# Two sequences per turn in place of one in TensorE's loop over the six local-attention layers

## The reference, cut to what matters

```
for i in range(DEPTH):            # DEPTH = 6, HEADS = 16, DIM_HEAD = 64, WINDOW = 32
    x = attn_layer(shift_tokens(x), Wqkv[i], q_scale[i], k_scale[i], Wo[i]) + x
    x = ffn_layer(shift_tokens(x), ln_g[i], ln_b[i], W1[i], b1[i], W2[i], b2[i]) + x
# attn_layer: qkv = x @ Wqkv; l2-normalised q, k with scaled rotary tables;
#   softmax over a window of 32 + 32 keys; (attention @ v) @ Wo
# ffn_layer: layer norm; a, gate = split(xn @ W1 + b1); (a * gelu(gate)) @ W2 + b2
```

## Time and profile before

| what | value |
|---|---|
| median of 3 executions | 4560.43 us (4554.09 to 4564.13) |
| span of the profiled execution, first to last instruction | 4548.5 us |
| TensorE's loop over the layers | 92 turns, from 1535.8 to 4461.2 us |
| TensorE busy with matmuls, over the whole span | 87% |

### The profile page before, as it was taken

How to read it: one execution, slowest core, us unless ns; L and a number is a source line. 1 busy time by engine, 2 the same in 40 slices (tenths; PEclk the granted TensorE clock), 3 DMA queues, 4 the chain that set the end, 5 groups by cost and what they waited for, 6 DMA issues and landing times. The chain is left out here.

```text
span 4548.5 us, 193033 instructions
## 1 busy us (share of the span) xinstructions
PE 3976.9 (87%) x73440; PEld 3313.4 (73%) x73441; DVE 3489.3 (77%) x6491; ACT 3343.1 (73%) x6195; POOL 2757.1 (61%) x3194
## 2 busy tenths in 40 slices
PE   7999845656556899999999999999999999999998
PEld 4555424544435788888888888888888888888886
DVE  6888352223336799999999999999999999999994
ACT  4777423333324799889998999899998999899995
POOL 3333252332235677777776777677776777677772
PEclk9999877777777999999999999999999999999999
DMA  4000322421211111121112111121112211121111
GB/s 159 1 0 0 81 86 100 149 75 63 91 42 50 46 44 51 40 71 47 44 47 61 50 50 44 45 68 45 47 48 58 55 45 44 44 68 48 47 44 39
DMA packets 141379, 254.22 MB, mean 56 GB/s; under 512 B 33984, under 2 KB 56640, under 8 KB 136640
## 3 DMA queue, kind: packets, MB, share of 16 engines
q1 hardware_dynamic: 133088, 235.11, 17.9%
q0 software_dynamic: 8192, 17.84, 1.3%
HBM read 70.38 MB, written 44.04 MB: 25 GB/s over the span
## 5 line engine op out<-in xcount | busy, mean ns | idle before, releaser
L2723 POOL TENSOR_TENSOR d_rc<-d_rc,d_rs 128x512 f32<-128x512 f32 x768 | 967.6, 1282 | 314.2 <-DVE d_rs L2806 277.3
L2733 POOL TENSOR_TENSOR d_rc<-d_rc,d_inv 128x1024 f32<-128x1024 f32 x384 | 723.1, 1904 | 127.7 <-DVE d_inv L2827 127.7
L2540 ACT ACTIVATE d_sq<-d_pair 128x512 f32<-128x512 f32 x768 | 454.3, 592 | 237.6 <-DVE d_rs L2806 141.8
L2293 PE MATMUL d_pair<-d_W_high,d_xs_high 128*128 128x512 f32 x1152 | 523.7, 455 | 96.7 <-issue 41.4
L2806 DVE TENSOR_TENSOR d_rc<-d_pair,d_rot 128x512 f32<-128x512 f32 x768 | 525.1, 684 | 15.4 <-ACT d_sq L2540 8.8
L2806 DVE TENSOR_TENSOR d_rs<-d_pair,d_rot 128x512 f32<-128x512 f32 x768 | 523.2, 681 | 0.0
L2293 PE MATMUL d_pair<-d_W_low,d_xs_high 128*128 128x512 f32 x1152 | 462.3, 401 | 1.2 <-issue 1.2
L2293 PE MATMUL d_pair<-d_W_high,d_xs_low 128*128 128x512 f32 x1152 | 461.2, 400 | 0.0
L2816 DVE TENSOR_REDUCE d_ss<-d_sq 128x16 f32<-128x1024 f32 x384 | 448.3, 1209 | 0.0
L2834 DVE TENSOR_REDUCE d_mx<-d_pair 128x16 f32<-128x1024 f32 x192 | 235.0, 1224 | 217.4 <-PE d_pair L2379 217.4
L2440 PEld LDWEIGHTS d_pair<-d_OT,d_Wo 128*128 128x128 f32 x3072 | 373.5, 192 | 18.5 <-issue 1.5
(11 more groups left out here) (404 smaller groups left out, 10362.6 us busy)
## 6 DMA issues: line engine op xcount, KB each, us to landing
d_VW<-d_V SPq DMA_DIRECT2D x768, 128.0 KB, 2.4
d_VW<-d_V SPq DMA_DIRECT2D x576, 64.0 KB, 2.0
leaf_rows<-a_zeros SPq DMA_DIRECT2D x12, 1152.0 KB, 14.6
q_xrow<-leaf_rows SPq DMA_DIRECT2D x24, 576.0 KB
leaf_out<-q_yrow SPq DMA_DIRECT2D x24, 512.0 KB, 2.6
d_W_whole<-Wqkv_dram SPq DMA_DIRECT2D x7, 1536.0 KB, 6.5
f_xrow<-leaf_rows SPq DMA_DIRECT2D x8, 576.0 KB, 3.6
b_table<-q_w_dram SPq DMA_DIRECT2D x4, 1024.0 KB, 7.9
```

Of the source, the lines that this page charges most:

```text
L2293: mm = nc.tensor.matmul(target, x_part[:, t.par, :], w_part[:, c, :], start=n == 0, stop=n == 2)
L2540: nc.scalar.activation(sq[:, half, 512 * j:512 * j + 512], ps[:, j, :], ACT.Square).then_inc(s[f"s{qk}{j}_ready"], 1)
L2723: nc.gpsimd.tensor_tensor(own[:, :, a, :], own[:, :, a, :], other[:, :, 1 - a, :], ALU.add).then_inc(s[f"add{qk}_ready"], 1)
L2733: nc.gpsimd.tensor_tensor(heads(rc[:, t.par, half, :]), heads(rc[:, t.par, half, :]), inv[:, t.par, half, :].unsqueeze(2).to_broadcast([12 ...
```

## The change

A new driver, and TensorE is run by it. The same slots run in the same order with the same waits; a turn of the loop now holds four slots in place of two, and there are 46 turns in place of 92. The eight slots ahead of the loop and the eight behind it stay as they are, and so do the drivers of the other engines.

```diff
+        def run_in_pairs(eng, slot):
+
+            def peeled(l, b):
+                for par in range(2):
+                    slot(lambda behind: Tile(l, b, par, behind))
+
+            for b in range(UNROLLED):
+                peeled(0, b)
+            with eng.Fori(UNROLLED // 2, LAYERS * SEQS // 2) as two:
+                for odd in range(2):
+                    for par in range(2):
+                        slot(lambda behind: FlatTile(two * 2 + odd, par, behind))
+            for b in range(UNROLLED):
+                peeled(LAYERS, b)
...
-            run_flat(pe, slot)
+            run_in_pairs(pe, slot)
```

## The result

The changed kernel took 5408.12 us at the median (5397.98 to 5427.45) against 4562.28 for the kernel before, beside it: a ratio of 1.186, 95% interval 1.184 to 1.1876, 846 us more. The forecast was 5190, with a range to 5290. The direction held, the size didn't: 627 us were foreseen, and 5408 lies above the range.

What follows compares the result with a forecast made beforehand. TensorE was taken to bound the layer loop. Slots +377, turn ends +293, less 6 and 17 for branches and 20 for split-weight waits, gave +627 us on the 4560 median: 5190 us, range 5000 to 5290.

Steps and rivals of the forecast that it cites:

- The bound: In the layer loop TensorE, busy for 2802 of 2886 us, sets the time; VectorE is in lock step with it.
- A: Rival: the instruction store holds the new turn, so only branches go: -6 us, 4554 us; chance 0.06.
- B: Rival: held turn as in A, VectorE's chain keeps out of the way, full 0.37 us gained: -17 us, 4543; chance 0.03.
- C: Rival: fetching is hidden inside a turn and only the branch misses: +146 us, 4706 us; chance 0.05.
- D: Rival: some packets stay, or the missed target comes with its successor: 5085, 5065 or both 4960 us; chance together 0.16.
- the head's second stop: Packet ends 14 instructions behind the loop's head, at the turn's fifth matmul: a further stop of 2.8 us.
- signs named: Expected in the new trace: 11 to 13 packets a turn, issue stops of 2 to 2.5 us, turns of about 77 us.
- 182 x 2.07 = +377 us: Loop slots running as first-time code, each 2.07 us longer from fetch stops; bounds +127 to +564 us.
- the three slots: Full slots in first-time code, 16.22, 18.62 and 17.93 us, mean 17.59 against 15.52 in the loop.
- The turn's end: At 45 taken branches to packets not held, stops of 3.75 and 2.8 us, 6.5 us together: +293 us.
- The value of a branch: At 46 removed turn ends, 0.37 us each, of which VectorE's chain takes 0.24 back: 0.13 us, 6 us in all.
- waits for split weights: At a layer's first tiles a late TensorE finds weights ready: some 4 us at five places, -20 us.

Runs made afterwards that it cites:

- the rotated kernel: The kernel before, two slots to a turn, with its loop cut mid-slot behind the turned keys so the branch hides behind issued matmuls: 4344.51 us against 4346.97, ratio 0.999.

## Why the prediction was wrong in size

**Right.** The bound, and that TensorE's stops have no cover. The mechanism: a turn of 11.3 packets is read anew each time, no packet of it stays, and the rivals with a held turn (A, B), hidden fetching (C) and packets kept by their place (D) are out: 13 of 13 touched packets came in each turn, with stops. The place of the head's second stop, to the instruction. Of the signs named, 13.0 packets to a turn came (11 to 13 foreseen); the turn is 82 us and not 77, its start has 4.8 us of stops and not 6. That a stop is a delivery less the time of the packet before.

**The term that was missing.** The prediction said of the slots "182 x 2.07 = +377 us" and priced no change of the clock at all; it took the 0.99 of the earlier trace rows along. The stops take TensorE's clock to its lower level, and the matmuls behind them cost 1.30 us a slot, +233 us. The two kernels with idle time and no fetching show that the idle time does it. The rows were read for their gaps alone. The granted clock fell to 0.50 at the last two of these stops, which end at 4475.62 and 4479.49, and stayed there for 6.8 us, as this row of the kernel before has it (the clock is the last column but two):

```profile
4478.10:4484.90 6.80, 5.35 (x51) 4.91 (x51) 2.66 (x5) 3.19 (x7) 0.00 (x0) 0.50 0.01 2
```

What hid the term is that the three slots of which the 2.07 us was taken all ran at 1.00; the stretch of the earlier trace rows around them had 0.96.

**Terms that were mis-sized.** The stops inside slots: 2.07 us a slot foreseen. Measured are 2.90 with the head's second stop, which is 1.15 us a turn or 0.29 a slot; the rest is 2.61 against the 2.07, 180 x 2.61 = 470 us against 377. The three slots that the mean came from had one stop of 0.72 us in the first, two in the second (1.16 us at 1538.48, and the one below, which the earlier trace rows leave out) and one in the third:

```profile
1553.52 0.24 PE L2412 MATMUL d_pair<-d_VW,d_PT 64*32 64x64 f32 x1 [1.82 <-issue]
```

The stop at 1538.48 is the head's second stop, and the prediction counts it twice: in the mean of the slots and again at the turn's end. Without it the mean is 2.07 - 1.16 / 3 = 1.7 us, so stops inside slots were taken too small by 0.9 us. The turn has five places for them, four of 2.0 to 2.5 us, and the fifth, near 2574, in two turns of three, wasn't counted.

The turn's end: 6.5 us foreseen, 0.92 x 4 + 1.15 = 4.8 measured, since the second stop was 1.2 us over the usual step in place of 2.8, 45 x 4.8 = 217 us against 293. The head of the turn runs at the lower clock, where the three steps ahead of this stop take 0.59, 0.43 and 0.43 us, some 0.7 us more than before: this covers part of the delivery, and the rest of the difference stays open.

**The small terms.** The value of a branch, 0.13 us of its 0.37 where VectorE's chain stands behind: 0.125 in the rotated kernel, with both slots at 15.46. At the first tiles of a layer 28.8 us of waits for split weights went whole, -29 in place of -20. The profile still puts 18.4 us at five places down to them, but at these places the missed branch ended between 0.2 us before and 0.4 us behind the writing of the weights (at 2040.91 us, weights at 2040.71, for one), so this is the stop at the branch.

The terms as measured, for 45 turns: 470 + 217 + 233, less the stops and waits that were there before (0.11 + 0.16 a slot, 49 us) and 36 for the two small rows of the table: 835 us, within a few us of the 837 above, which differ by rounding. Had the clock stood in the sum with the other terms as they were, it would have come to 4560 + 627 + 233 = 5420. That this is near 5408 is in part luck: the slots were 93 us too low and the turn ends 76 us too high.

## What to carry to other kernels

A loop of TensorE is free of fetching only while all packets of code that a turn touches are held: here up to 7 packets of 256 instructions, and no longer at 8, counted with loads, matmuls, waits and register work, and with where the head lies in its packet. Look at the queue of instructions in the profile over the loop: silent means held. At 12 and 13 packets dense runs of small matmuls stopped where packets end (2.0 to 2.5 us), a branch back cost a whole delivery (3.6 us), and both were paid a second time in the clock (1.3 us a slot). A branch of 0.2 us was better moved to where matmuls are queued (0.06% faster) than unrolled away (19% slower). And where stops are added to a busy engine, look at the granted clock behind the stops that the trace already has.

## What the runs showed of the hardware that was not expected

- An idle stretch of 2.7 us once in a turn of TensorE's otherwise busy loop is enough for matmuls at the 1.2 GHz level behind it, which cost 2.0 us a turn; behind 7.3 us they cost 2.3 us.
- At 8 touched packets a turn fetches either nothing or 9 packets, mostly by turns, with a stop of 4.5 to 5.2 us at the branch ahead of the 9. There two packets start within 0.1 to 1.0 us of each other, and the stop is longer than the 3.6 us of the changed kernel, where they start some 3 us apart; the turn of eight slots shows the same at its head (4.5 to 5.0 us). What decides between the two ways stays open.
- The head's place in its packet is worth 83 us in the changed kernel, 1.6%, without an instruction of difference in the turn.
